# A feed-forward chunk as three steps of the tracks' common order, with the gate multiplication moved to the next chunk's first step

## The chip, the cores and the metric

The kernel runs on one core of a Trainium2 chip. The metric is the device time of one execution in microseconds (us), median of several runs. The profile is of one execution.

## What is computed

Four layers, each an attention over a 77-row context and a feed-forward, each with a layer norm in front and a tanh-gated residual. The input x is four streams of 512 x 128, float32. Cut to the feed-forwards that the change touches:

```python
x = x + tanh(g_ffn[0]) * _L0_ffn_ref(_layernorm(x), ...)   # 8 chunks of 128 hidden units, relu
x = x + tanh(g_ffn[1]) * _L1_ffn_ref(_layernorm(x), ...)   # 4 experts, F = 512, top 2
x = x + tanh(g_ffn[2]) * _L2_ffn_ref(_layernorm(x), ...)   # 8 experts, F = 352, top 2
# inside L1 (L2 is alike): all experts are computed, the gates are zero for those not chosen
h = silu(einsum('td,edf->etf', xf, w1)) * einsum('td,edf->etf', xf, w3)
expert_out = einsum('etf,efd->etd', h, w2)
out = einsum('te,etd->td', gates, expert_out)
```

The attentions are A0, A1, A2 (16 heads; A1 first computes a temperature for each head from the statistics of all scores) and A3 (one head). The fourth feed-forward, F3, has 8 linear experts.

## The kernel before

**Two tracks.** The work is written as units: ("A", 0..19) and ("F", 0..11), four of each kind, one for each stream. Units A0 to A11 are attentions of the kinds A0, A1, A2; A12 to A19 are A3 and F3 in turn. Units F0 to F3 are of kind F0, F4 to F7 of kind F1 and F8 to F11 of kind F2. Every unit is a generator of steps on every engine (pre, body, tail), and `turns()` fixes one order of the letters A and F. `run()` walks that same order on each engine: at an A it issues the next step of the attention track on that engine, at an F the next step of the feed-forward track. So the order is a fixed program order on PE (TensorE), ACT (ScalarE), DVE (VectorE) and POOL alike, and every wait at the head of a queue holds all that stands behind it. `merged()` makes the order: each step has a weight, and the track whose weighted share done is smaller goes next.

**What runs beside what.** F unit i is merged with attention i + 2; F10 with units A12 to A15 (A3, F3, A3, F3) and F11 with A16, A17. A18 and A19 run alone at the end. The `pre` steps of the next F unit are spread over the steps of the present one.

**A chunk of F1 or F2.** F1 has 16 chunks a unit (4 for each of 4 experts), F2 has 24 (3 for each of 8 experts, 128, 128 and 96 wide); over eight units that is 160 chunks. One step of the F track is one whole chunk. On PE (L1571 and after) it issues "up" into bank 4 (three matmuls, L1542 to L1544, the helper `exact`), "gate" into bank 5 (the same three lines) and "down" (L1554, eight instructions into bank 7) for the chunk two before (`LATE = 2`). On ACT it issues the tanh of up into hb (L951). On DVE it issues silu, that is (hb + 1) * bank 4 (L1244), then the gate multiplication hb * bank 5 (L1248), and, where the chunk two before ends an expert, `gated` (L1233, four instructions: x + weight * bank 7). hb has three buffers. Bank 4 comes free with silu, bank 5 with the gate multiplication, bank 7 with `gated`:

```python
exact(bank[bu][0:m, :], wu, wul, xf_hi[s], xf_lo[s]).then_inc(*chunk_psum.up(u, n, "up"))
reader[bu] = (chunk_silu, u, n)
free(bg)
exact(bank[bg][0:m, :], wg, wgl, xf_hi[s], xf_lo[s]).then_inc(*chunk_psum.up(u, n))
reader[bg] = (chunk_ready, u, n)
if n >= LATE:
    down(n - LATE)
yield
```

**A chunk of F0** is one step as well: up (L1527), the relu on ACT (L943), down of the chunk before (L1521); DVE has nothing there.

**Attention steps** hold the projections (L1352, L1101), sixteen score blocks (PE L1364 and L1372, maxima on DVE L1109; kind A1 also exponentials on ACT L863 or L861, squares on POOL, sums on DVE L1117 and L1120), the temperature network of A1 (L1390 to L1398), sixteen heads (PE L1481, exp on ACT L917, PE L1466) and the output projection. F3's steps are three matmuls (L1595) and four DVE instructions (L1262).

Of the kernel before, what the change touches and what calls it, by code (L numbers as in the profile page):

```python
# [33 lines left out]
ALU = mybir.AluOpType  # L34
# [34 lines left out]
C0 = M0 * I0 // P  # L69
# [481 lines left out]
def main(nc, a, out, v):  # L551
# [125 lines left out]
    TURN = (4, 5)  # L677
# [22 lines left out]
    def steps_body(k):  # L700
        if k in MHA:
            return H + 1
        return {"A3": 3, "F0": C0 + 1, "F3": len(tiles)}.get(k) or len(chunks[k]) + LATE

    def steps_tail(k):
        return 7 if k in MHA else 2 if k == "F0" else 0
# [9 lines left out]
    def steps_f(u):  # L716
        return steps_body(kind(u)) + steps_tail(kind(u))


    beside = [[i + LAG] for i in range(ATTENTIONS - LAG)] + [[12, 13, 14, 15], [16, 17]]  # L720

    def turns():

        yield from "A" * len(weights_a(("A", 0)))
        yield from merged(weights_a(("A", 1)), [1.0] * steps_pre("F0"))
        for i in range(ATTENTIONS):
            yield from merged([w for j in beside[i] for w in weights_a(("A", j))], [1.0] * steps_f(("F", i)))
        for j in (18, 19):
            yield from "A" * len(weights_a(("A", j)))

# [28 lines left out]
    with nc.Block() as block:  # L759
# [49 lines left out]
        def _(act):  # L809
# [97 lines left out]
            def body(u):  # L907
# [30 lines left out]

                if k == "F0":
                    for c in range(C0):  # L940
                        act.wait_ge(*chunk_psum.at(u, c))
                        room_in(c)
                        act.activation(hb[c % 3], bank[TURN[c % 2]][:], ACT.Relu, scale=f0_cols[:, 0, c:c + 1],  # L943
                                       bias=f0_cols[:, 1, c:c + 1]).then_inc(*chunk_act.up(u, c))
                        yield
                    yield
                if k in chunks:
                    for n, (e, i, o, m) in enumerate(chunks[k]):
                        act.wait_ge(*chunk_psum.at(u, n, "up"))
                        room_in(n)  # L950
                        act.activation(hb[n % 3][0:m, :], bank[TURN[0]][0:m, :], ACT.Tanh, scale=0.5).then_inc(*chunk_act.up(u, n))  # L951
                        yield
                    for _ in range(LATE):
                        yield
                if k == "F3":
                    for _ in tiles:
# [21 lines left out]
        def _(dve):  # L978
# [218 lines left out]
            def body(u):  # L1197
# [26 lines left out]
                    yield  # L1224
                    return
                if k == "F0":
                    for c in range(C0 + 1):
                        yield
                def gated(e):

# [5 lines left out]

                if k in chunks:
                    todo = chunks[k]
                    for n in range(len(todo) + LATE):
                        if n < len(todo):  # L1240
                            e, i, o, m = todo[n]
                            h = hb[n % 3][0:m, :]
                            dve.wait_ge(*chunk_act.at(u, n))
                            dve.scalar_tensor_tensor(out=h, in0=h, scalar=1.0, in1=bank[TURN[0]][0:m, :], op0=ALU.add, op1=ALU.mult) \  # L1244
                                .then_inc(*chunk_silu.up(u, n))
                            dve.wait_ge(*chunk_silu.at(u, n))
                            dve.wait_ge(*chunk_psum.at(u, n))
                            dve.tensor_tensor(h, h, bank[TURN[1]][0:m, :], ALU.mult).then_inc(*chunk_ready.up(u, n))  # L1248
                        if n >= LATE and ends_expert(k, n - LATE):
                            gated(todo[n - LATE][0])  # L1250
                        yield
# [35 lines left out]
        def _(pe):  # L1287
# [167 lines left out]
            def body(u):  # L1455
# [60 lines left out]
                if k == "F0":  # L1516
# [7 lines left out]
                    for c in range(C0):  # L1524
                        d = TURN[c % 2]
                        free(d)
                        pe.matmul(bank[d][:], f0_in[:, c * P:(c + 1) * P], xf[:], start=True, stop=True) \  # L1527
                            .then_inc(*chunk_psum.up(u, c))
                        reader[d] = (chunk_act, u, c)
                        if c >= 1:  # L1530
                            down(c - 1)
                        yield
                    down(C0 - 1)
                    ffn_psum.counts[(u, "end")] = ffn_psum.counts[(u, C0 - 1)]
                    reader[7] = (oT_ready, u)
                    yield
                if k in chunks:
# [23 lines left out]
                    for n, (e, i, o, m) in enumerate(todo):  # L1561
# [7 lines left out]
                            pe.wait_ge(*xf_low.at(u))  # L1569
                        exact(bank[bu][0:m, :], wu, wul, xf_hi[s], xf_lo[s]).then_inc(*chunk_psum.up(u, n, "up"))  # L1570
                        reader[bu] = (chunk_silu, u, n)  # L1571
                        free(bg)
                        exact(bank[bg][0:m, :], wg, wgl, xf_hi[s], xf_lo[s]).then_inc(*chunk_psum.up(u, n))
                        reader[bg] = (chunk_ready, u, n)
                        if n >= LATE:
                            down(n - LATE)
                        yield
                    for n in range(len(todo) - LATE, len(todo)):
                        down(n)
                        if n + 1 == len(todo):  # L1580
                            ffn_psum.counts[(u, "end")] = ffn_psum.counts[(u, n)]
                        yield
# [88 lines left out]
```

## Time and profile before

| | |
|---|---|
| median of 3 runs | 1237.0 us (1235.21 to 1238.47) |
| profiled execution | 1225.93 us, span 1224.2 us |
| PE busy | 987.4 us, 81% |
| DVE busy | 713.9 us, 58% |
| ACT busy | 462.0 us, 38% |
| mean granted TensorE clock | 0.891 |
| chain that ended last | PE 54%, DVE 27%, ACT 9% |

Busy time is the time in which an engine has an instruction under way. The granted clock is a share of TensorE's full clock. The chain is followed back from the last instruction through whatever released each step. "Idle before, releaser" is the time in which an engine's queue stood still ahead of an instruction, and the instruction that ended it. The feed-forward units of kinds F1 and F2 lie between about 420 and 1180 us; about 113 to 420 us belongs to F0.

### The profile page before, as it was taken

Reading aid. Unit: us, or ns where it says so; the run is one execution under the profiler, and the core shown is the slowest. Engines: PE = TensorE matmul, PEld = TensorE weight load, DVE = VectorE, ACT = ScalarE, POOL = GpSimd, SP = SyncE. Lnnn points to the kernel's source line nnn. Section 1 sums busy time; section 2 is a strip of 40 time slices with the busy share of each in tenths; the row PEclk is TensorE's granted clock in tenths of the full one; section 3 lists DMA queues with packets and bytes.
Section 4 is the critical chain, followed back from the end, with each engine's and each line's share of the span. In section 5 each row is a group of like instructions: output and inputs, shape, how many; then the busy total and the mean of one; then the engine's idle time right before and its main releaser. Section 6 shows DMA issues by size and latency. Waiting matters only on the chain.

```text
span 1224.2 us, 14483 instructions
## 1 busy us (share of the span) xinstructions
PE 987.4 (81%) x4795; PEld 659.0 (54%) x4795; DVE 713.9 (58%) x2190; ACT 462.0 (38%) x1101; POOL 105.7 (9%) x175
## 2 busy tenths in 40 slices
PE   3477988986877877876889889989989888789866
PEld 2333443443332565464566656667667666567754
DVE  1853351438183594496365665756765677666755
ACT  2334435457476354454425316315315211212210
POOL 2100000003030130021000100100100100000000
PEclk9678999988696897898889989989989988989987
DMA  9200000000000000000000000000000000000000
GB/s 270 82 1 1 1 1 0 1 1 1 1 1 1 1 1 0 1 1 1 1 1 1 1 1 1 2 0 1 1 1 1 1 1 9 1 9 1 1 9 9
DMA packets 12065, 12.72 MB, mean 10 GB/s; under 512 B 3758, under 2 KB 7896, under 8 KB 11992
## 3 DMA queue, kind: packets, MB, share of 16 engines
q10 hardware_dynamic: 5536, 8.04, 2.2%
q1 hardware_dynamic: 6072, 3.24, 1.0%
q0 software_dynamic: 384, 0.53, 0.2%
q8 instruction: 39, 0.64, 0.2%
q14 instruction: 34, 0.28, 0.1%
HBM read 10.75 MB, written 1.05 MB: 10 GB/s over the span
## 4 chain that ended last, share of the span: by engine, by line
PE 54%; DVE 27%; ACT 9%; issue 4%; POOL 1%; POOLq 0%; ACTq 0%; DVEq 0%
PE bank L1554 7%; PE bank L1542 5%; PE bank L1466 5%; PE bank L1544 5%; PE bank L1543 5%; DVE hb L1244 4%; PE bank L1352 4%; PE bank L1481 3%; DVE nm L1109 3%; DVE x L1262 3%; DVE hb L1248 3%; DVE x L1233 2%; ACT PTs L917 2%; ACT hb L951 2%; PE bank L1319 2%
## 5 line engine op out<-in xcount | busy, mean ns | idle before, releaser
L951 ACT ACTIVATE hb<-bank 96x512 f32<-96x512 f32 (+1 forms) x160 | 95.2, 595 | 337.7 <-PE bank L1544 337.5
L1244 DVE SCALAR_TENSOR_TENSOR hb<-hb,bank 96x512 f32<-96x512 f32 (+1 forms) x160 | 109.2, 682 | 184.1 <-ACT hb L951 183.6
L1554 PEld LDWEIGHTS bank<-m_w,hb 128*128 128x128 f32 (+1 forms) x1280 | 178.7, 203 | 23.4 <-issue 3.5
L1554 PE MATMUL bank<-m_w,hb 128*128 128x128 f32 (+1 forms) x1280 | 180.0, 286 | 0.4
L1542 PE MATMUL bank<-parts,m_w_lo 128*96 128x512 f32 (+1 forms) x320 | 155.1, 485 | 14.9 <-DVE hb L1244 14.9
L1543 PE MATMUL bank<-parts,m_w_hi 128*96 128x512 f32 (+1 forms) x320 | 137.4, 429 | 0.0
L1544 PE MATMUL bank<-parts,m_w_hi 128*96 128x512 f32 (+1 forms) x320 | 137.2, 429 | 0.0
L1248 DVE TENSOR_TENSOR hb<-hb,bank 96x512 f32<-96x512 f32 (+1 forms) x160 | 109.7, 686 | 5.5
L1364 PE MATMUL bank<-KT,Qs 96*128 96x308 f32 x192 | 78.2, 426 | 42.0 <-ACT PTs L863 21.2
L1481 PE MATMUL bank<-Qs,KT 112*77 112x512 f32 x192 | 95.6, 529 | 16.4 <-ACT PTs L917 14.3
L1542 PEld LDWEIGHTS bank<-parts,m_w_lo 128*96 128x96 f32 (+1 forms) x320 | 64.8, 203 | 52.8 <-DVE hb L1244 20.7
L1109 DVE TENSOR_REDUCE nm<-bank 128x4 f32<-128x308 f32 x192 | 83.7, 469 | 14.7 <-PE bank L1368 7.8
L985 DVE RECIPROCAL rden<-bank 128x16 f32<-128x16 f32 x48 | 12.2, 254 | 123.5 <-PE bank L1305 123.5
L775 POOL TENSOR_SCALAR rstd_a<-mv_a 128x4 f32<-128x4 f32 x20 | 4.6, 228 | 900.5 <-DVE mv_a L1004 900.5
L1364 PEld LDWEIGHTS bank<-KT,Qs 96*128 96x128 f32 x192 | 36.3, 192 | 73.0 <-ACT PTs L863 30.5
L1544 PEld LDWEIGHTS bank<-parts,m_w_hi 128*96 128x96 f32 (+1 forms) x320 | 65.0, 203 | 18.8 <-issue 0.5
L1543 PEld LDWEIGHTS bank<-parts,m_w_hi 128*96 128x96 f32 (+1 forms) x320 | 65.3, 204 | 13.3 <-issue 3.9
L1352 PE MATMUL bank<-xfa,WqR 128*96 128x512 f32 x96 | 55.3, 696 | 9.7 <-ACT xfa L825 4.7
L1233 DVE SCALAR_TENSOR_TENSOR x<-bank,gw,x 128x128 f32<-128x128 f32 x192 | 53.8, 342 | 12.7 <-PE bank L1554 12.7
L1466 PE MATMUL bank<-PTs,VP 77*32 77x512 f32 x384 | 59.3, 663 | 0.0
L1481 PEld LDWEIGHTS bank<-Qs,KT 112*77 112x77 f32 x192 | 29.0, 156 | 51.4 <-ACT PTs L917 32.1
L794 POOL TENSOR_TENSOR PTs<-PTs 128x308 f32<-128x308 f32 x64 | 44.5, 701 | 98.3 <-ACT PTs L863 71.4
(271 smaller groups left out, 1543.5 us busy)
## 6 DMA issues: line engine op xcount, KB each, us to landing
m_w<-in_L_ffn_w_dram ACTq DMA_DIRECT2D x2, 1024.0 KB, 11.3
nat_m<-in_L_ffn_W_dram ACTq DMA_DIRECT2D x1, 1408.0 KB, 16.8
x<-in_x_dram SPq DMA_DIRECT2D x4, 256.0 KB, 7.8
out_dram<-x SPq DMA_DIRECT2D x4, 256.0 KB, 2.0
f_out<-in_L_ffn_Wout_dram POOLq DMA_DIRECT2D x8, 64.0 KB, 7.7
m_w<-in_L_ffn_W_experts_dram ACTq DMA_DIRECT2D x1, 512.0 KB, 16.8
ctxn<-in_ctx_dram SPq DMA_DIRECT2D x4, 38.5 KB
Wq<-in_L_xattn_Wq_dram SPq DMA_DIRECT2D x2, 64.0 KB
```

The costliest lines, as they stand in the source:

```text
L951: act.activation(hb[n % 3][0:m, :], bank[TURN[0]][0:m, :], ACT.Tanh, scale=0.5).then_inc(*chunk_act.up(u, n))
L1109: dve.tensor_reduce(nm[:, t, J * g:J * g + J], bank[RING[(G + n) % 3]][:, 0:J * S2].rearrange("p (h k) -> p h k", k=S2), AX.X, ALU.max, ne ...
L1244: dve.scalar_tensor_tensor(out=h, in0=h, scalar=1.0, in1=bank[TURN[0]][0:m, :], op0=ALU.add, op1=ALU.mult) \
L1248: dve.tensor_tensor(h, h, bank[TURN[1]][0:m, :], ALU.mult).then_inc(*chunk_ready.up(u, n))
L1352: pe.matmul(bank[b][0:QK, :], WqR[l][:, g, :], xf[:], start=True, stop=True).then_inc(*q_psum.up(u, g))
L1364: op = pe.matmul(dst, Qs[0:QK, g, t * P:(t + 1) * P], KT[0:QK, J * g:J * g + J, :].rearrange("p h k -> p (h k)"), start=True, stop=l == 1)
L1466: op = pe.matmul(bank[2 + g % 2][32 * j:32 * j + 32, :], VP[:, h, :], PT[h % NPT][0:S2, :], start=True, stop=True, tile_position=(0, 32 * j))
L1481: pe.matmul(dst, KT[:, h, :], Qs[0:QK + H, h // J, :], start=l != 0, stop=True).then_inc(*scores_psum.up(u, h))
L1542: pe.matmul(dst, w_lo, x_hi, start=True, stop=False)
L1543: pe.matmul(dst, w_hi, x_hi, start=False, stop=False)
L1544: return pe.matmul(dst, w_hi, x_lo, start=False, stop=True)
L1554: op = pe.matmul(bank[7][:, t * P:(t + 1) * P], hb[n % 3][0:m, t * P:(t + 1) * P], wd, start=i == 0 and t == 0, stop=ends_expert(k, n) and ...
```

## The change

The step counts of F0, F1 and F2 grow: two steps for each chunk of F0, three for each chunk of F1 and F2 (up, gate, down), and three for each of the two trailing steps. `weights_f` gives them weights in `merged()`. Each engine's body yields between the parts: on PE up, gate and down are in steps of their own; on ACT the tanh stands in the second of the three; on DVE silu and `gated` stand in the third, and the gate multiplication of chunk n in the first step of chunk n + 1, behind `gated` and behind whatever attention step comes between. No instruction is added or taken away, no buffer or bank changes, and what each instruction waits for is the same.

```diff
-        return {"A3": 3, "F0": C0 + 1, "F3": len(tiles)}.get(k) or len(chunks[k]) + LATE
+        return {"A3": 3, "F0": 2 * (C0 + 1), "F3": len(tiles)}.get(k) or 3 * (len(chunks[k]) + LATE)
...
+    def weights_f(u):
+
+        k = kind(u)
+        if k == "F0":
+            return [0.9, 0.9] * (C0 + 1) + [1.0] * steps_tail(k)
+        return [0.7, 0.7, 1.1] * len(chunks[k]) + [0.1, 0.1, 1.1] * LATE
...
-            yield from merged([w for j in beside[i] for w in weights_a(("A", j))], [1.0] * steps_f(("F", i)))
+            yield from merged([w for j in beside[i] for w in weights_a(("A", j))], weights_f(("F", i)))
...
                     for n, (e, i, o, m) in enumerate(chunks[k]):
+                        yield
                         act.wait_ge(*chunk_psum.at(u, n, "up"))
                         room_in(n)
                         act.activation(hb[n % 3][0:m, :], bank[TURN[0]][0:m, :], ACT.Tanh, scale=0.5).then_inc(*chunk_act.up(u, n))
                         yield
-                    for _ in range(LATE):
+                        yield
+                    for _ in range(3 * LATE):
                         yield
...
+                    def gate(n):
+                        m = todo[n][3]
+                        h = hb[n % 3][0:m, :]
+                        dve.wait_ge(*chunk_silu.at(u, n))
+                        dve.wait_ge(*chunk_psum.at(u, n))
+                        dve.tensor_tensor(h, h, bank[TURN[1]][0:m, :], ALU.mult).then_inc(*chunk_ready.up(u, n))
+
                     for n in range(len(todo) + LATE):
+                        if 0 < n <= len(todo):
+                            gate(n - 1)
+                        yield
+                        yield
                         if n < len(todo):
...
-                            dve.wait_ge(*chunk_silu.at(u, n))
-                            dve.wait_ge(*chunk_psum.at(u, n))
-                            dve.tensor_tensor(h, h, bank[TURN[1]][0:m, :], ALU.mult).then_inc(*chunk_ready.up(u, n))
                         if n >= LATE and ends_expert(k, n - LATE):
...
                         exact(bank[bu][0:m, :], wu, wul, xf_hi[s], xf_lo[s]).then_inc(*chunk_psum.up(u, n, "up"))
                         reader[bu] = (chunk_silu, u, n)
+                        yield
                         free(bg)
                         exact(bank[bg][0:m, :], wg, wgl, xf_hi[s], xf_lo[s]).then_inc(*chunk_psum.up(u, n))
                         reader[bg] = (chunk_ready, u, n)
+                        yield
                         if n >= LATE:
                             down(n - LATE)
                         yield
```

F0's body on ACT and PE gets one more yield for each chunk in the same way, and the trailing steps of all kinds get theirs.

## Rows read from the trace of the kernel before

**Rows 1.** The page: span, busy time of the engines, chain by engine

```profile
span 1224.2 us, 14483 instructions
PE 987.4 (81%) x4795; PEld 659.0 (54%) x4795; DVE 713.9 (58%) x2190; ACT 462.0 (38%) x1101; POOL 105.7 (9%) x175
...
PE 54%; DVE 27%; ACT 9%; issue 4%; POOL 1%; POOLq 0%; ACTq 0%; DVEq 0%
```

**Rows 2.** Windows: length, busy PE, PEld, DVE, ACT, POOL, then granted clock, DMA

```profile
113.00:420.00 307.00, 250.58 (x962) 121.24 (x963) 141.46 (x458) 160.66 (x401) 36.26 (x55) 0.85 0.00 1
420.00:490.00 70.00, 53.00 (x253) 41.07 (x252) 49.61 (x136) 34.21 (x111) 11.22 (x16) 0.85 0.00 0
490.00:560.00 70.00, 55.88 (x286) 39.76 (x287) 50.49 (x134) 33.67 (x117) 13.09 (x19) 0.93 0.00 1
560.00:685.00 125.00, 104.97 (x541) 73.09 (x539) 64.15 (x193) 50.86 (x90) 3.22 (x5) 0.90 0.00 1
685.00:1010.00 325.00, 290.85 (x1579) 214.97 (x1578) 215.14 (x610) 109.03 (x199) 18.47 (x34) 0.95 0.00 1
1010.00:1180.00 170.00, 138.78 (x736) 109.20 (x735) 120.19 (x367) 31.62 (x59) 6.31 (x10) 0.91 0.02 5
1180.00:1224.00 44.00, 30.76 (x141) 19.56 (x139) 20.55 (x79) 4.21 (x9) 1.25 (x2) 0.77 0.02 6
```

**Rows 3.** Waits of PE from 420 to 1180 us: total, times, longest

```profile
PE bank L1319 <- DVE xna L1014: 18.3, 8, 5.9
PE bank L1542 <- DVE hb L1244: 14.9, 13, 3.3
PE bank L1390 <- DVE feat L1154: 11.3, 2, 6.8
PE bank L1364 <- ACT PTs L863: 10.3, 10, 2.3
...
PE bank L1364 <- DVE Qs L1101: 8.1, 8, 3.3
```

**Rows 4.** Waits of DVE from 420 to 1180 us

```profile
DVE hb L1244 <- ACT hb L951: 181.8, 103, 4.7
```

**Rows 5.** Timeline of one F2 chunk beside A2's score blocks: start, us, engine

```profile
724.15 0.50 PE L1542 MATMUL bank<-parts,m_w_lo 128*128 128x512 f32 x1
...
724.95 0.39 PE L1542 MATMUL bank<-parts,m_w_lo 128*128 128x512 f32 x1
...
725.15 0.60 ACT L951 ACTIVATE hb<-bank 128x512 f32<-128x512 f32 x1 [5.29 <-PE bank L1544]
...
725.65 1.05 PE L1554 MATMUL bank<-m_w,hb 128*128 128x128 f32 x8
725.78 0.69 DVE L1244 SCALAR_TENSOR_TENSOR hb<-hb,bank 128x512 f32<-128x512 f32 x1 [1.61 <-ACT hb L951]
...
726.46 0.39 PE L1364 MATMUL bank<-KT,Qs 96*128 96x308 f32 x1
...
728.77 0.50 PE L1542 MATMUL bank<-parts,m_w_lo 128*128 128x512 f32 x1
```

**Rows 6.** Timeline of DVE, an F1 chunk beside two score blocks of A1

```profile
440.04 0.68 DVE L1244 SCALAR_TENSOR_TENSOR hb<-hb,bank 128x512 f32<-128x512 f32 x1
440.75 0.69 DVE L1248 TENSOR_TENSOR hb<-hb,bank 128x512 f32<-128x512 f32 x1
...
444.00 0.68 DVE L1244 SCALAR_TENSOR_TENSOR hb<-hb,bank 128x512 f32<-128x512 f32 x1
```

**Rows 7.** Timeline at the end of A1's score blocks, before its temperature network

```profile
463.36 0.69 DVE L1244 SCALAR_TENSOR_TENSOR hb<-hb,bank 128x512 f32<-128x512 f32 x1 [2.57 <-ACT hb L951]
...
469.61 0.80 PE L1390 MATMUL bank<-feat,t_w1b 128*64 128x16 f32 x6 [4.45 <-DVE feat L1154]
```

**Rows 8.** Timeline: an expert's end on DVE (gated), and five F3 steps on DVE

```profile
736.95 1.12 DVE L1233 SCALAR_TENSOR_TENSOR x<-bank,gw,x 128x128 f32<-128x128 f32 x4
...
1078.23 7.57 DVE L1262 SCALAR_TENSOR_TENSOR x<-bank,gw,x 128x128 f32<-128x128 f32 x20 [0.42 <-PE bank L1595]
```

More of the change, by code:

```diff
@@ L1226, in body @@
                 if k == "F0":
-                    for c in range(C0 + 1):
+                    for _ in range(steps_body(k)):
                         yield
@@ L1529, in body @@
                         reader[d] = (chunk_act, u, c)
+                        yield
                         if c >= 1:
@@ L1532, in body @@
                         yield
+                    yield
                     down(C0 - 1)
@@ L1571, in body @@
                         reader[bu] = (chunk_silu, u, n)
+                        yield
                         free(bg)
@@ L1574, in body @@
                         reader[bg] = (chunk_ready, u, n)
+                        yield
                         if n >= LATE:
@@ L1578, in body @@
                     for n in range(len(todo) - LATE, len(todo)):
+                        yield
+                        yield
                         down(n)
```

## The prediction

> **What bounds the kernel now.** I read the page first: PE is busy 987.4 of 1224.2 us and carries 54% of the chain, DVE 27%, ACT 9% [rows 1]. So PE is the engine to fill, and what can be won by an order alone is its idle time and its slow clock. The windows by stage say where the idle time is (length less PE busy) [rows 2]. It is 56.4 us in F0's stage (113 to 420), 31.1 us where F1 runs beside A1 (420 to 560), 20.0 us where F1 runs beside A2 (560 to 685), 34.2 us where F2 runs beside A2 (685 to 1010), 31.2 us where F2 runs beside A3 and F3 (1010 to 1180), and 13.2 us in the tail, where no F step is left. From 420 to 1180 that is 116.5 us, and with F0's stage 172.9 us.
>
> The waits say who holds PE from 420 to 1180 [rows 3]. Only 14.9 us of it is a chunk's up waiting for silu to free bank 4. The rest is the attention track: transposes that wait for a normalised x (18.3 us), the temperature network (11.3 us in two waits), score blocks that wait for exponentials (10.3 us) or for queries (8.1 us), and some fifteen smaller ones. The waits of DVE show why some of these are late: DVE stands 181.8 us, 103 times, in front of silu for a tanh [rows 4], and all attention work behind it stands too. Where PE is the bound this costs nothing. The timeline shows a place where it costs: DVE waits 2.57 us for a tanh, then has the router and the temperature statistics to do, and PE waits 4.45 us for them [rows 7].
>
> **The pace of a chunk.** One F2 chunk takes PE from 724.15 to 726.46, that is 2.31 us: up 0.80, gate 0.70, down 0.81 [rows 5]. Then attention blocks follow until 728.77. PE has no gap here, so this pattern stays PE-bound at 4.62 us whatever the order. Beside A1's score blocks the pattern is DVE's: silu comes every 3.96 us with DVE full in between [rows 6]. There too an order of the same instructions gives nothing. The change can win only in the rest: starts and ends of attentions, projections, heads, the temperature network.
>
> **What it removes.** Working the weights through `merged()`, the longest run of attention steps with no F step between falls from 6 to 3 (A1 beside F1), 4 to 2 (A2 beside F1), 3 to 1 (A2 beside F2), 3 to 2 and 2 to 1 (with A3 and F3). In such a run PE waits at each step for ACT or DVE, then it gets 2.31 us of chunk at once, of which a latency of some 1.5 us uses only a part. That latency is the row of the chunk itself: up is over at about 724.95, tanh starts at 725.15 and silu is done at 726.47, 1.52 us later [rows 5]. Cut in three pieces of 0.7 to 0.8 us, the same work covers two or three such waits. A wait that is longer than a whole chunk period is not shortened, since the F work for each attention step stays the same in total. I take a third of the 116.5 us, 39 us. The bounds are nothing (all waits are long or in full stretches) and two thirds, 78 us (all but the PE- and DVE-bound share). In F0's stage a chunk was already short and DVE has no part in it: a tenth of 56.4 us, 6 us, between nothing and 15. Together 45 us.
>
> The move of silu one or two attention steps back on DVE belongs to this. The tanh is then done when DVE comes to silu, and most of the 181.8 us of standing goes. By itself I price it at nothing: it is idle time of an engine that is not the bound, and its worth is already in the third.
>
> **What it adds.** No instruction, no DMA; POOL and SP get only empty steps. What is added is a tighter coupling of DVE to PE.
>
> First, plain chunks. Silu(n) must be over before up(n+1). With no attention step between, gate and down cover 1.51 us against the 1.52 us from tanh to silu's end [rows 5], so it just fits. But attention work of DVE now stands between up's step and silu's step, and only one step's slack is left where there were two or three. I take nothing for it, with 0.3 us at the 120 chunks that end no expert, 36 us, as the upper bound. The 0.3 us is half of one score block on PE (4 blocks between 726.46 and 728.77, 0.58 us each).
>
> Second, the 40 ends of experts with a chunk behind them (3 in each of 4 F1 units, 7 in each of 4 F2 units). `gated` waits for down(n-2) in the third step, holds DVE for 1.12 us [rows 8], and the gate multiplication of chunk n, 0.69 us [rows 6], now stands behind it. Counted from the start of gate(n): down is over at 1.51, `gated` runs from 1.6 to 2.7, one attention step of DVE follows (0.42 us for maxima), and the multiplication ends at about 3.85. PE wants bank 5 after down, one attention step (0.58), up (0.80) and none or one more attention step: at 2.9 or 3.5. So PE stands 0.4 to 1.0 us at each end. Beside F3 the attention step on DVE is 7.57 / 5 = 1.51 us [rows 8] and the stall is up to 1.8 us. Before, the multiplication stood ahead of `gated` and this wait did not exist. I take 0.65 us x 40 = 26 us, between 10 (a part falls into DVE-bound stretches) and 56 (the 28 ends of F2 at 1.8 us and the 12 of F1 at 0.45).
>
> **The sum.** 45 won less 26 lost is 19 us, against the profiled execution 1225.9 - 19 = 1206.9 us. The median of the runs, 1237.0, stands 11.1 us above the profiled execution, and what lies around the span there was 1.7 us. I put the difference on the median: 1237.0 - 19 = **1218 us**. The change of the busy totals is none, so PE should stay near 987 us unless its clock moves.
>
> **The clock.** It was granted at 0.95 from 685 to 1010, where PE was busy 89% of the time, and at 0.85 from 113 to 420 and from 420 to 490, at 82% and 76% [rows 2]. Fewer gaps should let it rise a little; I leave this out of the sum. The Trainium skill, page TensorE: Matmul & The Clock Gate, section "Part 1: The HAM clock gate", says that the half rate is the default and that activity releases the full one. By it the gain would be larger than the gaps alone; by the rows as summed it is 19 us. It is a rival below.
>
> **Rivals.**
> - *The ends of experts and the tighter coupling win (slower).* One mechanism: the gate multiplication comes late on DVE and PE stands at gate(n+1) for bank 5. For it: DVE is busy 66% and 71% in the two F2 windows [rows 2], and it has steps of 1.1 to 3 us from the attention side that would now stand between silu and the multiplication. Against it: PE's in-order waits on silu are only 14.9 us now. It decides where stalls pass what is recovered. With 1.0 us at 40 ends and only 15 us recovered it is +25 us, 1262 us; with equal sums nothing. Chance 0.28.
> - *Nothing to be had (same).* The stretches where PE or DVE is full set the time, the waits are long ones, and a smaller recovery, some 26 us, is eaten by the ends: 1237 us. For it: the longest waits (6.8, 5.9 us) are longer than a chunk [rows 3]. Chance 0.15.
> - *The clock rises too (much faster).* If the gaps closed are those that let the clock fall, PE's work from 420 to 1180 (643.5 us at 0.85 to 0.95) goes some 3% faster besides. That is another 19 us: 1199 us. Chance 0.15.
> - *My forecast,* 19 us less with no help from the clock: chance 0.42.
>
> **Range.** Below: two thirds recovered less 26 and the clock's help in part gives about -42 us, 1195. Above: the slower rival up to +16 us, 1253. The likeliest case by itself is 1208 to 1232, from a recovery of 32 to 55 us against 26. Faster by over 0.3% (3.7 us, about what a measurement of this kernel can tell from no change) 0.57, within it 0.15, slower 0.28.
>
> **What would show it.** Right, step by step: DVE's wait in front of silu falls from 181.8 us to under 80; PE's waits for exponentials, queries and the temperature network shrink; a new row appears in which the first matmul of gate waits for the gate multiplication, about 20 to 30 us in some 40 times, longest under 2 us; PE's idle time from 420 on falls by about 15 us net. Wrong: if that new row is well over 40 us, or up's wait for silu grows past 40 us, the coupling is worth more than I gave it; if DVE's standing vanishes and PE's attention waits stay as they are, they were never made by the coarse steps.

## The result

The change makes the kernel faster: 1192.1 us median (1191.43 to 1196.13, 4 runs) against 1236.11 us (1233.53 to 1238.47, 4 runs), ratio 0.9651, 95% interval 0.9622 to 0.9681. That is 44 us where 19 were forecast, and 3 us below the lower end of the range. In the experiments one execution, of the kernel with two steps a chunk, was in a slow state: it took 2916.9 us where its three others took 1174 to 1185, and it is left out there.

The page of the changed kernel, to hold against [rows 1]. PE, DVE and ACT do the same instructions as before.

```profile
span 1189.7 us, 14483 instructions
PE 977.7 (82%) x4795; PEld 639.2 (54%) x4795; DVE 707.1 (59%) x2190; ACT 461.5 (39%) x1101; POOL 105.3 (9%) x175
...
PE 54%; DVE 29%; issue 5%; ACT 5%; POOL 2%; POOLq 0%; ACTq 0%; DVEq 0%
```

The span is 34.5 us shorter (1224.2 to 1189.7). PE's idle time gives 24.8 us of it (236.8 to 212.0) and its busy time 9.7 us (987.4 to 977.7). The same instructions are busy for less time, which fits the mean granted clock (0.891 and 0.895). The other 9.5 of the 44 us are no difference between these two traces: the profiled execution of before, 1225.93 us, was a fast one and lies below all four runs of its median, while that of the changed kernel, 1191.43 us, is within 1 us of its median.

The waits of PE from 420 to 1180 us in the changed kernel, to hold against [rows 3]:

```profile
PE bank L1563 <- DVE hb L1255: 51.9, 48, 3.1
PE bank L1563 <- DVE hb L1266: 23.4, 28, 2.2
PE bank L1338 <- DVE xna L1025: 11.5, 5, 4.8
PE bank L1409 <- DVE feat L1165: 4.5, 2, 2.3
```

L1563 is the first matmul of up or gate (L1542 before), L1255 the gate multiplication, L1266 silu. PE's waits for attention work have nearly gone from this stretch: the temperature network had 11.3 us and has 4.5 (L1409). Score blocks waited 10.3 us for exponentials and 8.1 us for queries, and neither row is left among the first seven. In their place stand the forecast row, gate waiting for the gate multiplication, with 51.9 us in 48 times, and up waiting for silu, 23.4 us. So part of PE's waiting has only changed its place. From the first F1 unit to the end of the last F2 unit PE's waits for silu or the gate multiplication rise from 14.9 to 77.4 us and all its other waits fall from 96.3 to 13.4 us. DVE's standing in front of silu for a tanh, 181.8 us before [rows 4], is 97.3 us over the whole kernel, where under 80 was forecast:

```profile
DVE hb L1266 <- ACT hb L961: 97.3, 52, 3.5
```

**Where the time came from.** The windows below are cut where units begin: at the first layer-norm statistics on DVE of the attention that runs beside. After the length stand the busy times of PE, PEld (weight loads), DVE, ACT and POOL, then the granted clock. The rows are F0 beside A4 and A5, F1 beside A6 and A7 (kind A1), F1 beside A8 and A9 (kind A2), F2 beside A10 and A11, and F2 beside A12 to A17. First the kernel before, at these cuts:

```profile
264.60:407.70 143.10, 110.07 (x359) 51.03 (x358) 76.43 (x253) 88.31 (x262) 27.01 (x40) 0.76 0.00 1
407.70:606.90 199.20, 152.70 (x744) 109.50 (x743) 127.24 (x369) 93.74 (x278) 27.59 (x40) 0.88 0.00 1
606.90:769.10 162.20, 144.90 (x755) 103.06 (x754) 97.37 (x275) 59.56 (x108) 6.71 (x12) 0.93 0.00 1
769.10:961.10 192.00, 176.44 (x975) 130.13 (x974) 128.23 (x346) 68.34 (x125) 8.84 (x16) 0.96 0.00 1
961.10:1175.30 214.20, 177.70 (x942) 139.68 (x940) 153.50 (x477) 42.05 (x78) 10.48 (x18) 0.93 0.01 3
```

The changed kernel:

```profile
261.60:413.00 151.40, 115.76 (x359) 54.31 (x358) 77.40 (x253) 88.03 (x262) 26.95 (x40) 0.74 0.00 1
413.00:575.30 162.30, 136.33 (x745) 97.17 (x744) 124.98 (x370) 94.35 (x279) 27.55 (x40) 0.96 0.00 1
575.30:727.20 151.90, 143.31 (x755) 99.11 (x753) 95.27 (x275) 59.45 (x109) 6.79 (x12) 0.93 0.00 1
727.20:922.70 195.50, 176.79 (x974) 124.60 (x974) 126.50 (x346) 68.07 (x124) 8.53 (x16) 0.97 0.00 1
922.70:1139.60 216.90, 177.22 (x939) 136.84 (x939) 151.25 (x476) 41.88 (x77) 10.46 (x18) 0.94 0.01 4
```

The gain is in F1 beside kind A1: 199.2 to 162.3 us, 36.9 us less. F1 beside A2 gives 10.3 us. F2 loses 3.5 and 2.7 us, F0 beside A1 loses 8.3 us (most of it goes with the clock, see below), and F0 beside A2 and A3 gains 3.7 us (106.1 to 102.4). PE was idle 46.5 us in F1 beside A1 before and is idle 26.0 us now, and its granted clock went from 0.88 to 0.96, which takes 16.4 us from its busy time.

Inside the first of these two units (A6) one sees which part gave it. Windows of the kernel before: projections, score blocks, temperature network, heads and end.

```profile
407.70:423.90 16.20, 13.32 (x47) 7.88 (x45) 11.16 (x39) 6.40 (x20) 2.57 (x4) 0.81 0.01 2
423.90:455.00 31.10, 25.29 (x134) 21.18 (x135) 29.33 (x71) 16.56 (x73) 9.12 (x13) 0.95 0.00 1
455.00:478.10 23.10, 15.64 (x71) 12.69 (x69) 13.84 (x49) 9.88 (x24) 2.10 (x3) 0.70 0.00 0
478.10:507.70 29.60, 23.94 (x126) 14.48 (x126) 9.28 (x29) 14.04 (x23) 0.00 (x0) 0.91 0.00 1
```

The same four of the changed kernel:

```profile
413.00:424.60 11.60, 10.26 (x40) 5.91 (x38) 9.90 (x37) 6.69 (x20) 2.62 (x4) 0.94 0.00 1
424.60:456.00 31.40, 23.65 (x127) 19.19 (x125) 30.23 (x73) 18.16 (x79) 9.75 (x14) 0.95 0.01 1
456.00:469.80 13.80, 11.23 (x73) 8.73 (x71) 12.54 (x48) 8.15 (x18) 1.40 (x2) 1.00 0.00 1
469.80:494.30 24.50, 22.96 (x141) 14.79 (x141) 9.87 (x30) 14.32 (x25) 0.00 (x0) 1.00 0.00 1
```

The score blocks, which are DVE's (busy 29.33 of 31.10 us), stay at 31 us as forecast. All three other parts shrink: 4.6, 9.3 and 5.1 us. (The feed-forward work is spread a little differently over the parts: PE has 47 and 40 instructions in the first and 126 and 141 in the last.) In the temperature network the clock was at 0.70 and is at 1.00.

### The profile page after: what moved, and what is told of

The parts are those of the page before. It is cut to its first block, busy times and chain, and to the rows that moved or that the text cites. A ratio compares the mean times of both kernels' runs of the same rounds, so it can differ in the third digit from the quotient of the medians.

```text
span 1189.7 us, 14483 instructions
## 1 busy us (share of the span) xinstructions
PE 977.7 (82%) x4795; PEld 639.2 (54%) x4795; DVE 707.1 (59%) x2190; ACT 461.5 (39%) x1101; POOL 105.3 (9%) x175
## 4 chain that ended last, share of the span: by engine, by line
PE 54%; DVE 29%; issue 5%; ACT 5%; POOL 2%; POOLq 0%; ACTq 0%; DVEq 0%
PE bank L1575 9%; PE bank L1563 5%; PE bank L1485 4%; PE bank L1565 4%; DVE hb L1255 4%; PE bank L1564 4%; PE bank L1371 3%; DVE nm L1120 3%; DVE x L1244 3%; PE bank L1500 3%; DVE x L1281 3%; DVE hb L1266 2%; PE bank L1540 2%; PE bank L1546 2%; DVE Z L1131 2%
## 5 line engine op out<-in xcount | busy, mean ns | idle before, releaser
L1563 PE MATMUL bank<-parts,m_w_lo 128*96 128x512 f32 (+1 forms) x320 | 156.6, 489 | 75.9 <-DVE hb L1255 51.9
L1575 PEld LDWEIGHTS bank<-m_w,hb 128*128 128x128 f32 (+1 forms) x1280 | 169.8, 200 | 26.9 <-issue 14.1
L1266 DVE SCALAR_TENSOR_TENSOR hb<-hb,bank 96x512 f32<-96x512 f32 (+1 forms) x160 | 108.7, 679 | 97.6 <-ACT hb L961 97.3
L1563 PEld LDWEIGHTS bank<-parts,m_w_lo 128*96 128x96 f32 (+1 forms) x320 | 60.7, 190 | 138.1 <-DVE hb L1255 77.7
L1565 PE MATMUL bank<-parts,m_w_hi 128*96 128x512 f32 (+1 forms) x320 | 130.9, 409 | 0.0
L1564 PE MATMUL bank<-parts,m_w_hi 128*96 128x512 f32 (+1 forms) x320 | 130.8, 409 | 0.0
L1255 DVE TENSOR_TENSOR hb<-hb,bank 96x512 f32<-96x512 f32 (+1 forms) x160 | 108.9, 681 | 8.2 <-PE bank L1565 6.2
L1383 PE MATMUL bank<-KT,Qs 96*128 96x308 f32 x192 | 81.6, 442 | 17.9 <-ACT PTs L870 10.3
L996 DVE RECIPROCAL rden<-bank 128x16 f32<-128x16 f32 x48 | 12.2, 255 | 129.1 <-PE bank L1324 128.8
L1244 DVE SCALAR_TENSOR_TENSOR x<-bank,gw,x 128x128 f32<-128x128 f32 x192 | 53.9, 343 | 42.1 <-PE bank L1575 42.0
L1565 PEld LDWEIGHTS bank<-parts,m_w_hi 128*96 128x96 f32 (+1 forms) x320 | 61.0, 191 | 17.0
L1564 PEld LDWEIGHTS bank<-parts,m_w_hi 128*96 128x96 f32 (+1 forms) x320 | 61.4, 192 | 7.4 <-issue 3.5
L1383 PEld LDWEIGHTS bank<-KT,Qs 96*128 96x128 f32 x192 | 39.4, 206 | 44.2 <-ACT PTs L870 17.5
L1281 DVE SCALAR_TENSOR_TENSOR x<-bank,gw,x 128x128 f32<-128x128 f32 x128 | 44.7, 350 | 19.1 <-PE bank L1620 14.7
L1485 PE MATMUL bank<-PTs,VP 77*32 77x512 f32 x384 | 54.7, 624 | 0.0
L824 ACT ACTIVATE Os<-bank 128x512 f32<-128x512 f32 x48 | 28.7, 597 | 64.8 <-PE bank L1485 64.8
## 6 DMA issues: line engine op xcount, KB each, us to landing
m_w<-in_L_ffn_w_dram ACTq DMA_DIRECT2D x2, 1024.0 KB, 11.3
```

Source lines behind the costliest of these rows:

```text
L1383: op = pe.matmul(dst, Qs[0:QK, g, t * P:(t + 1) * P], KT[0:QK, J * g:J * g + J, :].rearrange("p h k -> p (h k)"), start=True, stop=l == 1)
L1485: op = pe.matmul(bank[2 + g % 2][32 * j:32 * j + 32, :], VP[:, h, :], PT[h % NPT][0:S2, :], start=True, stop=True, tile_position=(0, 32 * j))
L1563: pe.matmul(dst, w_lo, x_hi, start=True, stop=False)
L1564: pe.matmul(dst, w_hi, x_hi, start=False, stop=False)
L1565: return pe.matmul(dst, w_hi, x_lo, start=False, stop=True)
L1575: op = pe.matmul(bank[7][:, t * P:(t + 1) * P], hb[n % 3][0:m, t * P:(t + 1) * P], wd, start=i == 0 and t == 0, stop=ends_expert(k, n) and ...
```

## The experiments

The time of before in each group is that of its own runs beside it: 1238.03 us for the first four, 1228.07 us for the next four, 1227.52 us for the last two. So ratios are compared across groups, and times within one. The kernel of the next paragraph, the reference of much that follows, has the ratio 0.9337 in the first group; three kernels of the second group that differ little from it have 0.9387 to 0.9404. So 0.006 across the groups is no finding. Each edit is against the changed kernel, but for the two headed "in the kernel before"; "..." stands for lines left out.

**The multiplication back behind silu.** The three steps stay; the gate multiplication stands in the third step, ahead of `gated`.

```diff
-                        if 0 < n <= len(todo):
-                            gate(n - 1)
                         yield
                         yield
                         if n < len(todo):
                             ...
                                 .then_inc(*chunk_silu.up(u, n))
+                            gate(n)
```

> The changed kernel with the gate multiplication put back right behind silu, in the chunk's third step and ahead of gated; the three steps stay. Theory A (the order in three steps does it; the moved multiplication only adds the 52 us in which PE stands at gate for bank 5): the wait at gate for the multiplication falls from 51.9 us to under 20, and the kernel is as fast as the changed one or faster, 1170 to 1192 us. Theory B (the moved multiplication is needed, because silu and multiplication together, 1.37 us, stand in front of attention work on DVE): slower than the changed kernel by over 5 us.

Measured: 1154.41 us (1148.18 to 1164.84), ratio 0.9337, interval 0.9278 to 0.9395. That is 38 us faster than the change. The three steps by themselves (with F0's two, and with the tanh and silu in their later places) are worth 84 us, and the moved multiplication takes back nearly half of it. Its page, and the wait that is left at the first matmul of up or gate (L1264 is silu here; no wait for the multiplication is among the long ones):

```profile
span 1146.4 us, 14483 instructions
...
PE 948.7 (83%) x4795; PEld 624.8 (54%) x4795; DVE 714.8 (62%) x2190; ACT 460.7 (40%) x1101; POOL 105.6 (9%) x175
...
PE bank L1562 <- DVE hb L1264: 35.9, 38, 3.1
```

Against before, PE's idle time is 39.1 us less (236.8 to 197.7) and its busy time 38.7 us less (987.4 to 948.7). The stages, the same five as above:

```profile
257.20:407.00 149.80, 111.70 (x358) 51.77 (x357) 77.69 (x252) 88.20 (x262) 27.00 (x40) 0.78 0.00 1
407.00:576.10 169.10, 137.43 (x745) 98.52 (x744) 126.74 (x370) 93.55 (x278) 27.61 (x40) 0.96 0.00 1
576.10:721.90 145.80, 136.32 (x755) 95.91 (x754) 96.95 (x275) 59.30 (x109) 6.92 (x12) 0.98 0.00 1
721.90:901.70 179.80, 172.45 (x974) 123.86 (x974) 128.05 (x346) 68.01 (x124) 8.57 (x16) 0.99 0.00 1
901.70:1096.90 195.20, 168.37 (x939) 130.20 (x939) 153.55 (x477) 41.93 (x77) 10.47 (x18) 0.98 0.01 4
```

F2 now gains too, 12.2 and 19.0 us against before, where the change lost 3.5 and 2.7. PE is busy 172.45 of 179.80 us beside A10 and A11, at a clock of 0.99. F2 is where the moved multiplication cost most: 15.7 and 21.7 us between the two kernels.

**The move alone, in the kernel before.** One step a chunk; the multiplication of chunk n at the start of step n + 1 on DVE.

```diff
+                    def gate(n):
...
                     for n in range(len(todo) + LATE):
+                        if 0 < n <= len(todo):
+                            gate(n - 1)
                         if n < len(todo):
                             ...
                                 .then_inc(*chunk_silu.up(u, n))
-                            dve.wait_ge(*chunk_silu.at(u, n))
-                            dve.wait_ge(*chunk_psum.at(u, n))
-                            dve.tensor_tensor(h, h, bank[TURN[1]][0:m, :], ALU.mult).then_inc(*chunk_ready.up(u, n))
```

> The kernel before with one part of the change alone: chunks stay one step, the gate multiplication of chunk n moves to the start of step n + 1 on DVE. Theory A (three steps do it): no gain, 1230 to 1245 us. Theory B (the moved multiplication does it, since attention work on DVE gets in 0.69 us earlier): a good part of the 44 us, 1200 to 1225 us.

Measured: 1297.18 us (1295.25 to 1311.24), ratio 1.052 (1.0454 to 1.0585). The second half of the change alone makes the kernel slower by 5%, where neither theory had a loss of more than 7 us. In one coarse step, gate(n+1) comes right behind up(n+1), while the multiplication of chunk n stands on DVE behind the whole round of attention work. The wait of gate for it (L1548 for L1244 here):

```profile
PE bank L1548 <- DVE hb L1244: 95.5, 66, 4.8
```

**Silu and multiplication late, in the kernel before.** As the last, with silu moved to the next step's start as well.

```diff
+                    def gate(n):
...
                     for n in range(len(todo) + LATE):
-                        if n < len(todo):
-                            e, i, o, m = todo[n]
-                            ...  # silu and gate multiplication of chunk n
+                        if 0 < n <= len(todo):
+                            e, i, o, m = todo[n - 1]
+                            ...  # silu of chunk n - 1
+                            gate(n - 1)
```

> The kernel before, chunks stay one step, but silu and the gate multiplication of chunk n both move to the start of step n + 1 on DVE, so that DVE never stands long for a tanh (183.6 us before). Theory C (DVE standing for tanh with attention work behind it is what made PE wait): the wait in front of silu falls under 60 us and the kernel gains most of the 44 us, 1195 to 1215 us. Theory A (it is PE's own order, the chunk in one piece of 2.3 us): the wait falls, the time stays within 10 us of before or grows, as up now waits for a late silu: 1230 to 1260 us.

Measured: 1358.87 us (1346.17 to 1364.38), ratio 1.0966 (1.0902 to 1.1029). DVE hardly stands for a tanh any more, and up stands for silu instead:

```profile
PE bank L1547 <- DVE hb L1251: 145.0, 95, 5.5
...
DVE hb L1251 <- ACT hb L951: 34.4, 28, 3.1
```

So 149 us less of standing on DVE (183.6 to 34.4) came with 121 us more. Theory C as stated falls: taking the standing away does not by itself make the kernel faster. What the standing costs is not separated here, since the late silu brings a large wait of its own. The cost was above the 1260 us that theory A allowed for.

**PE in three steps, ACT and DVE early.** Up, gate and down in steps of their own; the tanh and silu in the first, the multiplication in the second, `gated` in the third.

```diff
                     for n, (e, i, o, m) in enumerate(chunks[k]):
-                        yield
                         act.wait_ge(*chunk_psum.at(u, n, "up"))
                         ...
+                        yield
                         yield
                         yield
...
                     for n in range(len(todo) + LATE):
-                        if 0 < n <= len(todo):
-                            gate(n - 1)
-                        yield
-                        yield
                         if n < len(todo):
                             ...
                                 .then_inc(*chunk_silu.up(u, n))
+                        yield
+                        if n < len(todo):
+                            gate(n)
+                        yield
                         if n >= LATE and ends_expert(k, n - LATE):
```

> The three steps on PE as changed, but ACT and DVE as early as before: the tanh in the first step beside up, silu in the first step on DVE, the gate multiplication in the second beside gate, gated in the third. So PE has the fine order and DVE still stands for tanh and for gate. Theory A (PE's fine order does it): keeps at least two thirds of the gain, 1190 to 1208 us. Theory C (DVE's standing was the cause): falls back to 1215 to 1240 us, with a wait in front of silu of over 150 us.

Measured: 1197.7 us (1189.45 to 1201.93), ratio 0.967 (0.9622 to 0.9717), inside theory A's bounds. DVE still stands 151.9 us in front of silu:

```profile
DVE hb L1262 <- ACT hb L960: 151.9, 109, 3.8
```

With the kernel of 1154 us this splits the 84 us of the three steps. 40 us come although silu stands early on DVE, so they come with PE's finer order. The other 43 us come when tanh, silu and multiplication move back behind one or two pieces of attention work, and only together with the fine order: with coarse steps the same kind of move cost 121 us.

**`gated` behind the multiplication.** The changed kernel with one thing different: `gated` moves to the next chunk's first step, behind the multiplication.

```diff
                         if 0 < n <= len(todo):
                             gate(n - 1)
+                        if n > LATE and ends_expert(k, n - 1 - LATE):
+                            gated(todo[n - 1 - LATE][0])
                         yield
                         yield
                         ...
-                        if n >= LATE and ends_expert(k, n - LATE):
+                        if n + 1 == len(todo) + LATE:
                             gated(todo[n - LATE][0])
```

> The changed kernel with gated moved behind the gate multiplication: both now stand in the next chunk's first step, the multiplication first. The three steps and the moved multiplication stay. Theory D (the moved multiplication costs by standing behind gated at the ends of experts, as the prediction had it): the wait at gate for the multiplication falls from 51.9 us to under 25 and the kernel comes to 1160 to 1180 us. Theory E (it costs by standing behind attention work anyway, at ends or not): 1185 to 1200 us, the wait stays over 40 us.

Measured: 1156.94 us (1150.14 to 1157.56), ratio 0.9404 (0.9354 to 0.9455), below theory D's 1160 (by the ratio it would be 1164 us in the group of 1238.03 us). By ratios that takes back 0.025 of the 0.031 that the moved multiplication cost, and the interval overlaps that of the kernel of 1154 us: with `gated` out of its way it costs nothing that shows. The timeline shows the mechanism at one place, the heads beside F2. In the changed kernel `gated` (L1244) waits for down, the multiplication (L1255) comes behind it and behind a division, and gate (the second L1563) stands 1.61 us. Rows of weight loads are left out here and in the next view:

```profile
815.81 0.69 DVE L1266 SCALAR_TENSOR_TENSOR hb<-hb,bank 128x512 f32<-128x512 f32 x1 [2.08 <-ACT hb L961]
816.11 1.06 PE L1575 MATMUL bank<-m_w,hb 96*128 96x128 f32 x8
816.93 0.48 PE L1563 MATMUL bank<-parts,m_w_lo 128*96 128x512 f32 x1
817.21 1.13 DVE L1244 SCALAR_TENSOR_TENSOR x<-bank,gw,x 128x128 f32<-128x128 f32 x4 [0.71 <-PE bank L1575]
...
818.74 0.68 DVE L1255 TENSOR_TENSOR hb<-hb,bank 128x512 f32<-128x512 f32 x1
...
819.47 0.48 PE L1563 MATMUL bank<-parts,m_w_lo 128*96 128x512 f32 x1 [1.61 <-DVE hb L1255]
```

The same place with `gated` behind: the multiplication is done when gate wants its bank.

```profile
796.76 1.06 PE L1577 MATMUL bank<-m_w,hb 96*128 96x128 f32 x8
...
797.56 0.68 DVE L1255 TENSOR_TENSOR hb<-hb,bank 128x512 f32<-128x512 f32 x1
797.58 0.48 PE L1565 MATMUL bank<-parts,m_w_lo 128*96 128x512 f32 x1
...
798.16 1.12 DVE L1244 SCALAR_TENSOR_TENSOR x<-bank,gw,x 128x128 f32<-128x128 f32 x4
798.35 0.41 PE L1565 MATMUL bank<-parts,m_w_lo 128*96 128x512 f32 x1
```

Over the kernel the wait of gate for the multiplication falls from 51.9 to 28.6 us (theory D had it under 25) and PE's idle time by 16.2 us (212.0 to 195.8), while its busy time falls by 25.1 us (977.7 to 952.6) and its clock rises from 0.895 to 0.918. Not all of the 51.9 us was at ends of experts. In 28 of the 48 waits, with 32.8 us, `gated` stands on DVE between silu and the multiplication that gate waits for; in the other 20, with 19.1 us, attention work alone does. In the kernel with `gated` behind, all 30 waits are of the second sort. Ten of the 48, with 12.0 us, lie in F1 beside A1, two of them (3.6 us) at ends of experts. The kernel of 1154 us has none of these ten, and its stage took 169.1 us against 162.3. A wait on PE costs nothing where DVE sets the pace, and that is the likely reason; the kernel with the multiplication moved only there (below) took 168.8 us.

**F0 in one step.** The kernel of 1154 us with F0's chunks as before.

```diff
-        return {"A3": 3, "F0": 2 * (C0 + 1), "F3": len(tiles)}.get(k) or 3 * (len(chunks[k]) + LATE)
+        return {"A3": 3, "F0": C0 + 1, "F3": len(tiles)}.get(k) or 3 * (len(chunks[k]) + LATE)
...
-            return [0.9, 0.9] * (C0 + 1) + [1.0] * steps_tail(k)
+            return [1.0] * steps_f(u)
...
```

> Three steps for F1 and F2 with the gate multiplication right behind silu (the kernel of 1154 us), but F0's chunks in one step with weight 1 as before. F0 beside the last two of its attentions (kind A1) took 143 us before and 150 us with two steps. If the two steps of F0 cause that, the stage goes back to about 143 us and the kernel to about 1147 us; F0 beside A0 loses up to its 3 to 6 us again. If the two profiles only differ by chance: 1150 to 1158 us and the stage at about 150 us.

Measured: 1162.93 us (1161.01 to 1163.97), ratio 0.9464 (0.9419 to 0.9508). The stage beside A1 stays at 149.7 us, so two steps of F0 do not cost there; the stage beside A2 and A3 goes back from 99.6 to 106.4 us. F0's part of the change is worth some 6 to 8 us (1162.93 against 1154.51 to 1156.94 us in the same group), and it shows beside kind A0.

**The multiplication moved only beside A1.**

```diff
+                    moved = k == "F1" and kind(("A", u[1] + LAG)) == "A1"
                     for n in range(len(todo) + LATE):
+                        if moved and 0 < n <= len(todo):
+                            gate(n - 1)
                         yield
                         yield
                         ...
-                            gate(n)
+                            if not moved:
+                                gate(n)
```

> Three steps with the gate multiplication right behind silu, except in the two F1 units that run beside attentions of kind A1, where it moves to the next chunk's first step as in the change. Their stage took 162 us with the moved multiplication and 169 us without. If the move is worth something where DVE is full and nothing where PE is: about 1147 us, the stage at 162 us. If the 7 us are chance or come from where the stage starts: 1150 to 1158 us.

Measured: 1155.26 us (1152.69 to 1157.97), ratio 0.9403 (0.9355 to 0.9451). The stage took 168.8 us, not 162, at a granted clock of 0.91 and with 23.4 us of PE idle; the changed kernel had it at 0.96 with 26.0 us idle. So the 7 us go with the clock of that execution and not with the moved multiplication, which neither gains nor costs there.

**Flat weights.** `weights_f` gives 1 for every step.

> Three steps with the gate multiplication right behind silu, with weight 1 for every feed-forward step (the weights of the change left out). If the finer order is what counts and not its exact weights: within 10 us of 1154 us. If the light weights of the trailing steps or the heavier down matter: over 1165 us.

Measured: 1154.51 us (1150.88 to 1159.03), ratio 0.9387 (0.9329 to 0.9445). The weights of the change do nothing that shows.

**`gated` one step later, multiplication behind silu.** The kernel of 1154 us with `gated` at the start of the next chunk's first step.

> Three steps, the gate multiplication right behind silu, and gated one step later, in the next chunk's first step, so that DVE comes to it when down is over (DVE stood 27.8 us, 15 times, in front of gated in the kernel of 1154 us). If the standing in front of gated costs PE anything: 1140 to 1150 us. If that standing is idle time that nothing needs: 1150 to 1160 us.

Measured: 1161.09 us (1149.63 to 1163.12), ratio 0.9465 (0.9397 to 0.9533). No gain, so nothing needed the time that DVE stood in front of `gated`.

**Two steps.** Up and gate together in the first, down in the second, with the gate multiplication behind silu.

```diff
-        return {"A3": 3, "F0": 2 * (C0 + 1), "F3": len(tiles)}.get(k) or 3 * (len(chunks[k]) + LATE)
+        return {"A3": 3, "F0": 2 * (C0 + 1), "F3": len(tiles)}.get(k) or 2 * (len(chunks[k]) + LATE)
...
-        return [0.7, 0.7, 1.1] * len(chunks[k]) + [0.1, 0.1, 1.1] * LATE
+        return [1.4, 1.1] * len(chunks[k]) + [0.2, 1.1] * LATE
...
                         reader[bu] = (chunk_silu, u, n)
-                        yield
                         free(bg)
...
```

> Two steps for a chunk of F1 and F2 instead of three: up and gate on PE in the first, down in the second; the tanh, silu, the gate multiplication and gated in the second step on ACT and DVE. It tells how much the cut between up and gate is worth. Theory A (each cut gives attention work a place, in proportion): about half way, 1180 to 1205 us. If it is mainly the later place of silu behind one round of attention work that frees DVE: 1155 to 1175 us. If attention work between up and gate is what hides tanh and silu from PE: over 1210 us.

Measured: 1180.54 us (1174.09 to 1185.47, 3 runs), ratio 0.9606 (0.9526 to 0.9686). There is no profile of these runs. The two cuts are thus worth 0.039 of the time for the first and, within wide intervals, 0.02 to 0.03 for the second (0.9606 against 0.9337 to 0.9404), with the shorter way of silu behind the tanh in it.

## Why the prediction was wrong

The direction was right, and the two sides of the sum were the right ones. The step that failed is the recovery, the term of 45 us. It measured 84 us, because a third of the idle time was too small a share and because the clock was left out of the sum at nothing. The cost at the ends of experts was too small as well: 26 us forecast, 38 us measured.

**The pace of a chunk and the full stretches: right, but laid over too much.** The score blocks of A1 keep their pace (31.1 and 31.4 us). A reason for taking only "a third of the 116.5 us" was that the pattern beside A1 is DVE's. I had drawn F1's windows at 420, 560 and 685, with A1 ending at 560, from the look of the rows. By units, F1 runs beside A1 until 606.9 and beside A2 until 769.1 (so the chunk of [rows 5], at 724.15, is one of F1 and not of F2), and PE's idle time beside A1 is 46.5 us, not 31.1. The DVE-bound score blocks are 31 of the 100 us of a unit. The other 69 us gave 19.0 us in A6 alone.

**The recovery: 45 us forecast, 84 us measured** when the multiplication stays behind silu. The profiled spans differ by 77.8 us (1224.2 to 1146.4), of which PE's idle time is 39.1 and its busy time, with the same instructions, 38.7. From 407 us on, the idle time falls by 40.6 us (115.9 to 75.3), which looks like the third that I took, 39. It is not quite that: a faster clock makes PE reach the same waits earlier and stand longer at them, so it hides part of what the order closes. What the clock is worth by itself can be read from the executions of one kernel. Of the 21 runs of before beside the experiments the longest span is 1238.6 us at a mean granted clock of 0.867 and the shortest 1218.7 us at 0.897; over all of them, each group about its own mean, a span is about 6 us shorter for each 0.01 of clock (3 to 8 us in single groups). From 0.891 to 0.918 that is some 16 us, an estimate. The other 60 us or so of the 77.8 are then the order's own, where 45 were forecast.

**The clock: a rival at 0.15, and what happened.** I wrote that fewer gaps "should let it rise a little; I leave this out of the sum". For the changed kernel that was nearly so, 0.891 to 0.895 in the two traces, and its 34.5 us are not the clock's in the main. In the kernel of 1154 us it rose to 0.918, and in the temperature network of A6 it rose from 0.70 to 1.00 with the change. That the order moved it is more than the chance of one execution: in the first group the kernel before had 0.867 to 0.882 in seven runs, the kernel of 1154 us 0.894 to 0.919 in four, and the slowest, with silu late, 0.838 to 0.865. The rule of the Trainium skill, page TensorE: Matmul & The Clock Gate, section "Part 1: The HAM clock gate", that activity releases the full rate, was the better guide; the traces of the kernel of 1154 us agree in all stages from 407 us on. One stage of the changed kernel does not show it: in F1 beside A2 PE's idle time halved (17.3 to 8.6 us) and the clock stayed at 0.93. F0 beside A4 and A5 shows how much chance there is in one stage. The kernels there have the same order, and the profiles differ: 151.4 us at 0.74, 149.8 us at 0.78, and with `gated` behind

```profile
258.90:402.50 143.60, 105.16 (x358) 48.64 (x357) 78.13 (x252) 88.26 (x262) 26.95 (x40) 0.82 0.00 1
```

143.6 us at 0.82, with PE idle 35.6, 38.1 and 38.4 us. From the first to the last, 10.6 us less of busy time came with 7.8 us less of length. This is also why 5 to 8 us between two profiles of a stage are no finding, and why the 8.3 us that F0 seemed to lose are not shown to be the change's.

**The ends of experts: right mechanism, too small.** The forecast row is there, 51.9 us in 48 times with 3.1 us the longest, where 20 to 30 us in 40 times under 2 us was said. Of it 28 waits with 32.8 us are at ends of experts; the other 20, behind attention work alone, the prediction did not have. By the test in the prediction (well over 40 us) the coupling was worth more than the 26 us I gave it: the change is 38 us slower than with the multiplication behind silu. Moving `gated` alone brings most or all of it back, as theory D had it. Of that kernel's 41.3 us of shorter span (1189.7 to 1148.4) 16.2 are idle time and 25.1 busy time; the clock's rise from 0.895 to 0.918 is worth some 14 us by the same estimate. The gaps beside A10 and A11 are 0.2 to 1.6 us each, where PE was otherwise full; beside A12 to A17 the longest is 3.1 us.

**The signs and the range.** PE's idle time over F1 and F2 fell by 22.9 us (115.9 to 93.0), where about 15 was said, and DVE's wait in front of silu to 97.3 us, not under 80. The range did not follow from its own bounds: two thirds recovered, 78 us, less 26 is 52 us before anything of F0 or the clock, so the lower end should have been 1185 us or less and not 1195. The slower rival's own price, 1262 us, lay outside the upper end as well. That 1192.1 us misses the range by 3 us is this slip; that 44 us came and not 19 is the recovery.

**Plain chunks: nothing taken, near right.** Up waits 23.4 us for silu in the changed kernel from 420 on, against 14.9 before, with 36 us as the upper bound of what it could add.

**DVE's standing: priced at nothing by itself.** No run removes the standing and nothing else. In the coarse order the edit that removed it made the kernel slower by 10%, as up then waited for silu. In the fine order the places of tanh, silu and multiplication are worth 43 us together, and the standing falls from 151.9 to 91.9 us with it.

**The slower rival** had the mechanism that the experiments found, and it did cut the gain nearly in half, but it did not decide, because the recovery was so much larger than the 15 us it assumed.

## What to carry to other kernels

Where one program order is fixed for all engines, cut a block of work into pieces no longer than the latencies beside it (here 0.7 to 0.8 us against 1.5 us), and put each dependent instruction far enough back that its input is ready, but ahead of anything that waits for later work: a 0.7 us multiplication behind a 1.1 us update that waits for a matmul cost most of 38 of 84 us. Test the cut and the move apart; here one was worth 84 us and the other cost 38. Price the clock by the spread of runs of one kernel before splitting a gain into idle and busy time, since a faster clock adds to the idle time. Cut windows where units begin, not where the rows seem to change.

## What the runs showed of the hardware

Over 21 runs of the kernel before, TensorE's mean granted clock lay between 0.867 and 0.897, and the span was shorter by about 6 us for each 0.01 more of clock (1238.6 us at 0.867, 1218.7 us at 0.897). A stage with the same instructions in the same order came out at granted clocks of 0.74, 0.78 and 0.82 in three profiled executions of different kernels, with 115.76, 111.70 and 105.16 us of busy time. In the temperature network TensorE was busy 15.64 of 23.10 us at a clock of 0.70, and 11.23 of 13.80 us at 1.00.
